# Attention with two pairs of score banks, and the value products between the two scores of a block

## The reference

```
Q = _l2norm(Q); K = _l2norm(K)                      # [batch, 16 heads, 1024, 8]
scores = jnp.einsum('bhqd,bhkd->bhqk', Q, K) * jax.nn.softplus(temp)
attn = jax.nn.softmax(scores, axis=-1)
out = jnp.einsum('bhqk,bhkd->bhqd', attn, V).transpose(0, 2, 1, 3).reshape(Bx, Tx, C)
return _lin(out, Wo, bo)
```

## Time and profile before

| what | value |
|---|---|
| runs shown, median (lowest to highest) | 1411.6 us (1411.15 to 1412.57) |
| the profiled execution, own time | 1414.99 us |
| its span, first to last instruction | 1413.2 us |
| mean granted clock of TensorE | 0.92 of 2.4 GHz |
| attention in the span | some 737 to 1243 us |
| ScalarE busy in 737 to 1243 | 475.94 us |
| TensorE busy in 737 to 1243 | 449.07 us |

### The profile page before, as it was taken

One profiled execution on the slowest core, in us unless ns is written; L12 is line 12 of the kernel. 1 busy time (PEld: TensorE's weight loads), 2 busy tenths in 40 slices (PEclk: granted clock), 3 DMA queues, 4 the chain that ended last, 5 costly groups with the idle time before them and its releaser, 6 DMA issues. The chain is left out here.

```text
span 1413.2 us, 18871 instructions
## 1 busy us (share of the span) xinstructions
PE 1121.0 (79%) x5854; PEld 404.7 (29%) x5854; DVE 835.6 (59%) x1017; ACT 990.6 (70%) x1057; POOL 325.5 (23%) x194
## 2 busy tenths in 40 slices
PE   5748787776899956774539998898999889869996
PEld 3213333332444422321531111111111111124443
DVE  5879998996566559995850432324143232456664
ACT  3767665653788821222439999999999999848885
POOL 3127676765011025654000000000000000011110
PEclk8769999998999979898759999999999999969999
DMA  2000001000100000000010111111011111000001
GB/s 72 0 16 30 30 34 55 30 30 30 31 30 30 30 24 0 0 0 8 0 32 4 35 32 23 22 23 29 19 35 29 23 22 23 14 32 31 30 30 60
DMA packets 24182, 36.28 MB, mean 26 GB/s; under 512 B 7362, under 2 KB 11970, under 8 KB 24130
## 3 DMA queue, kind: packets, MB, share of 16 engines
q1 hardware_dynamic: 24130, 35.71, 9.3%
HBM read 16.82 MB, written 6.29 MB: 16 GB/s over the span
## 5 line engine op out<-in xcount | busy, mean ns | idle before, releaser
L1612 ACT ACTIVATE att_prob<-att_s_ps 128x1024 f32<-128x1024 f32 x512 | 470.8, 1436 | 11.0 <-PE att_s_ps L1574 11.0
L1584 PE MATMUL att_o_ps<-att_prob,att_va 128*32 128x512 f32 x2048 | 277.8, 616 | 2.0 <-ACT att_prob L1612 2.0
L1574 PE MATMUL att_s_ps<-att_q_st,att_k_st 32*128 32x512 f16 x1024 | 194.2, 393 | 49.7 <-ACT att_prob L1612 12.2
L685 POOL TENSOR_TENSOR scan_hc<-scan_state,scan_c_rep 128x1024 f32<-128x1024 f32 x64 | 151.9, 2391 | 71.1 <-DVE scan_state L642 70.8
L1637 DVE RECIPROCAL hv_h_seq<-hv_h_seq 32x1024 f32<-32x1024 f32 (+1 forms) x20 | 105.3, 5265 | 84.3 <-DMA hv_h_seq<-hv_h_seq 84.3
L787 POOL TENSOR_TENSOR ffn_veps<-ffn_mv,all_eps 128x4 f32<-128x4 f32 x16 | 9.1, 569 | 605.4 <-DVE ffn_mv L944 605.4
L642 DVE TENSOR_TENSOR_SCAN scan_state<-scan_decay,scan_drive_ps 128x1024 f32<-128x1024 f32 x64 | 142.9, 2270 | 0.3 <-ACT scan_decay L615 0.3
L1574 PEld LDWEIGHTS att_s_ps<-att_q_st,att_k_st 32*128 32x128 f16 x1024 | 47.0, 91 | 334.7 <-ACT att_prob L1612 315.6
L1651 DVE COPY hv_h_seq<-att_o_ps 128x512 f32<-128x512 f32 x32 | 22.1, 691 | 200.4 <-PE att_o_ps L1584 200.4
L282 PE MATMUL scan_y_ps<-scan_hc,all_ident 128*128 128x512 f32 x256 | 127.5, 622 | 8.6 <-DVE scan_y_sb L661 6.2
L619 ACT ACTIVATE scan_c_rep<-scan_c_ps 128x1024 f32<-128x1024 f32 x64 | 65.5, 1023 | 79.3 <-PE scan_c_ps L282 79.1
(11 more groups left out here) (216 smaller groups left out, 1536.8 us busy)
## 6 DMA issues: line engine op xcount, KB each, us to landing
ffn_w_sel<-w_split SPq DMA_DIRECT2D x16, 512.0 KB, 3.2
w_split<-scan_w_parts SPq DMA_DIRECT2D x8, 512.0 KB, 2.9
att_q_st<-hv_part SPq DMA_DIRECT2D x64, 64.0 KB, 2.1
att_k_st<-hv_part SPq DMA_DIRECT2D x64, 64.0 KB, 2.1
hv_h_seq<-hv_h_seq SPq DMA_DIRECT2D x96, 32.0 KB
ln_x_half<-in_x SPq DMA_DIRECT2D x8, 256.0 KB, 2.9
scan_w_raw<-in_w1e SPq DMA_DIRECT2D x8, 256.0 KB, 3.0
scan_w_raw<-in_w2e SPq DMA_DIRECT2D x8, 256.0 KB, 3.3
```

The costliest lines, as they stand in the source:

```text
L685: pool.tensor_tensor(hc[:, n % 4, :], state[:, n % 2, :], c_rep[:, n % 4, :], ALU.mult).then_inc(weighed.sem, 1)
L1574: last = pe.matmul(s_ps[n % 3][:, i, :], k_st[rows, g % 2, kc * P:(kc + 1) * P], q_st[rows, g % 2, HALVES[half]], start=True, stop=True)
L1584: last = pe.matmul(o_ps[half][32 * j:32 * j + 32, :], va[:, g % 2, kc, j, :], prob[:, u % RING, j, :], start=kc == 0, stop=kc == KC - 1)
L1612: act.activation(prob[:, u % RING, 2 * pair:2 * pair + 2, :], s_ps[n % 3][:, :, :], ACT.Exp).then_inc(exped.sem, 1)
```

## The change

Two pairs of score banks are allocated instead of three, and a score waits for the exponential two back. The index of the pair is `n % 2`. On TensorE the value products of block `u - 2` stand between the first and the second pair of scores of block `u`, instead of behind both. Score 30 is in pair 0 under either rule, so VectorE reads pair 0 in every batch.

```diff
-        s_ps = [q.ps(f"s_ps{k}", [P, 2, HALF]) for k in range(3)]
+        s_ps = [q.ps(f"s_ps{k}", [P, 2, HALF]) for k in range(2)]
-        exped = q.count("exped", G * U * 2, 3)
+        exped = q.count("exped", G * U * 2, 2)
...
-                        pe.wait_ge(exped.sem, exped.before(b, n, 3 if n >= 2 else 2))
+                        pe.wait_ge(exped.sem, exped.before(b, n, 2))
                         if n == 2 * OUT_AT:
-                            project(b, n % 3)
+                            project(b, n % 2)
...
-                            last = pe.matmul(s_ps[n % 3][:, i, :], k_st[rows, g % 2, kc * P:(kc + 1) * P],
+                            last = pe.matmul(s_ps[n % 2][:, i, :], k_st[rows, g % 2, kc * P:(kc + 1) * P],
...
                         for u in range(U):
-                            for pair in range(2):
-                                scores(g, u, pair)
+                            scores(g, u, 0)
                             if (g, u) >= (0, 2):
                                 values(*divmod(g * U + u - 2, U))
+                            scores(g, u, 1)
...
-                                act.activation(prob[:, u % RING, 2 * pair:2 * pair + 2, :], s_ps[n % 3][:, :, :],
+                                act.activation(prob[:, u % RING, 2 * pair:2 * pair + 2, :], s_ps[n % 2][:, :, :],
...
-                        k = 0 if isinstance(b, int) and b == B - 1 else 2 * OUT_AT % 3
+                        k = 0
```

## The result

The changed kernel takes 1429.86 us (median of 4 runs, 1429.01 to 1430.96) where the kernel before takes 1412.09 us in the same session: slower by 17.8 us, a ratio of 1.0126 with a 95% interval of 1.0109 to 1.0144. The forecast was 1436.4, with 24.8 us more. Direction and mechanism held; the largest term of the sum was about twice what it measures.

The account below looks back on a forecast made before the run. ScalarE's exponentials, one per 0.917 us, were taken to bound attention. Per batch 4.35 + 0.92 + 0.52 + 0.40 = 6.19 us, 24.8 over four batches, gave 1436.4 us (own range 1430 to 1441; 8 in 10: 1419 to 1446).

Parts of the forecast that it names:

- the largest term of the sum: Steady blocks of attention: 29 late exponentials per batch at 0.15 us each, 4.35 us per batch.
- The turn over two blocks: Steady attention: second score 1.32 us after the first; two blocks take 3.82 us where ScalarE alone needs 3.67.
- The 0.51 and 1.02 are only seen with an idle ScalarE: Score-to-exponential start and exponential's length: with ScalarE still busy, they could shrink by up to 0.10 us, lateness to 0.05.
- By this part alone there is 0.25 us to spare, and no loss: Two pairs of banks alone: one pair's turn takes 1.58 us, ScalarE takes 1.83 for two exponentials.
- Start of a batch: First value products now stand ahead of number 5's scores, not number 6's: one exponential, 0.92 us per batch.
- Projection: At block 15, it has only exponential 29 to run beside it; stall 3.22 us against 2.70, 0.52 more.
- Restart: After the projection, exponential 31's score stands behind value products; 31 ends 2.85 us after score 30, 0.40 more.
- What would show it: Signs in the new trace: scores 1.32 us apart, ScalarE about 96% busy, some 30 stalls of 0.15 per batch.
- two pairs are enough: Rival, 0.06: second score runs beside the value products, only the projection's 2.1 us is left; 1413.7 us, no measurable change.
- Absorbed: Rival, 0.10: ScalarE takes late scores without the extra 0.10 us; only start, projection and restart cost 7.4; 1419.0 us.
- The clock falls more often: Rival, 0.12: TensorE idles a little more, one or two more slow-clock stretches per batch; 1442 to 1448 us.
- Faster: Rival, 0.02: exponentials could run at a shorter pace if TensorE and ScalarE got in each other's way before.

## Why the prediction was right, and what in it was wrong

- What bounds it: right. ScalarE's pace of 0.917 us sets attention in both kernels. Outside it the stretch ahead was 2.3 us shorter in this one execution, where no edit stands; the one behind it was the same to 0.1.
- The turn over two blocks: right, with 1.32 us between the scores, late in every fourth place, the block between with slack. Three pairs with the new order cost nothing, as the prediction said.
- Its size: wrong, and this is the term that made the sum too large. "The 0.51 and 1.02 are only seen with an idle ScalarE" was the right doubt with the wrong reason. All exponentials from which 0.51 could be read, in the earlier trace rows and at 30 in the earlier trace rows, are even ones, with a register instruction behind the scores' wait; the late ones are odd. The true price is 0.43, the lateness 0.075, and 29 x 0.075 x 4 = 8.7 us of 24.8 go. 16.1 are left, 16.6 are measured in attention. By terms a batch pays 29 x 0.075 = 2.2 for the turn where the sum had 4.35, and about 1.0 for the start, 0.6 for the projection and 0.3 for the restart, 4.1 together.
- "By this part alone there is 0.25 us to spare, and no loss": wrong. I drew the value products into the turn for the new order and left them out for the old one, where they stand ahead of the other score. Two pairs in the old order cost 27 us. The new order doesn't add to the loss, it takes some away: attention is 12.9 us shorter (519.8 to 506.9), of which 29 x 0.075 x 4 = 8.7 because the late exponential is an odd one now; most of the rest, 3.2, is the clock after the projection.
- Start of a batch: forecast 0.92 per batch. In the second batch the stall at number 5 is 1.27 against 0.43 at 6 before. With the next stall, at 7 or 8, which varies by up to 0.5, the four batches pay 0.84 to 1.23 in end-to-end distance; right within that.
- Projection: forecast 0.52, measured 3.18 - 2.59 = 0.59. Restart: forecast 0.40, measured 0.32; it is an odd exponential too, so its 0.51 was 0.43.
- What would show it: the claim of a ScalarE that is busy 96% was wrong, as told under the windows. The rest of the signs came as named, but for the size of 0.15.
- Rivals: *two pairs are enough* fell with the second score at 1.32 in every block. *Absorbed* came half true by size only: the late ones are there, and what is missing is not the 0.10 of overlap but the register instruction. *The clock falls more often* didn't happen in the changed kernel (1.00 in 776 to 856 and 893 to 981, 0.97 over attention in both kernels), though it did after the longer stall in the kernel with the old order. *Faster* had nothing for it.
- The Trainium skill's figures (ScalarE: Activation LUTs, What ACT_TABLE_LOAD costs) gave some 17 us, near the 17.8 measured, but not for their reason: they have the pace at 0.946 where the trace keeps 0.917, and the lateness at 0.08 by a pace that isn't there. The page's load of 1283 ns agrees with 1.28 in the rows above.
- The rule on rotating banks (the Trainium skill, Perfetto Trace Analysis, Matmuls) holds with a condition: with two pairs the evacuations kept their pace with 0.89 us of work queued ahead of every score, and lost it with 1.32 ahead of every second. Where the limit lies no run here tests; as an estimate from the chain of the changed kernel, 3 x 0.917 - 0.05 - 0.43 - 1.02 = 1.25 us.

## What to carry to other kernels

With buffers in rotation, don't compare the turn of one buffer with the pace; write down what stands in the in-order queue ahead of each refill, for each order of the queue, and close the chain until it meets itself. Where an engine waits for several semaphores, put the wait that comes last in time last in the source, so that register work and table loads are done ahead of it; here that alone gave 0.4%. A pair of buffers saved is dear if the lead that it gave was hiding something else: here it hid a value block, part of a loop's end, and part of a projection.

## What the runs showed of the hardware that I had not expected

- A register instruction between the arrival of the awaited result and the instruction that uses it: 0.08 us on ScalarE (0.51 against 0.43, in four kernels). Which exponentials have it, even, odd or none, follows from the waits' order and targets.
- An engine's row can be full while it loses 0.075 us in each fourth instruction.
- The end of a hardware loop costs ScalarE 2.37 to 2.71 us from its branch to its next instruction; how much of it is seen depends on how far the branch runs ahead of the engine's work.
- TensorE was busy 20.00 of 20 us at a granted clock of 0.50, with value products of 256 columns on strips of the array (745 to 765 above); the same work ran at 1.00 in 785 to 865. With half of the value products the clock was 0.50 in 900 to 1300. What decides between the two levels no run here shows.
